# Sorting stage of a graph-attention kernel: transfers spread over two issuing queues, and two instead of four values carried per edge

## The reference, cut to what matters

```
q = (x[src] @ qW); k = (x[dst] @ kW); v = (x[dst] @ vW)      # per edge, 4 heads of 24
e = exp(clip(sum_f q*k, -10, 10))                            # per edge and head
res[n] = sum over edges with src = n of  e / sum(e) * v
out = layernorm(x + (x + res))
```

## Time and profile before

| | us |
|---|---|
| median of 3 runs | 1697.75 (1695.93 to 1699.25) |
| profiled execution, its own time | 1694.7 |
| its span in the profile | 1692.6 |
| PE busy | 1471.8 (87%) |
| DVE busy | 1468.6 (87%) |
| ACT busy | 1013.3 (60%) |
| POOL busy | 1016.2 (60%) |

### The profile page before, as it was taken

One profiled execution on the slowest core, in us unless ns is written; L12 is line 12 of the kernel. 1 busy time (PEld: TensorE's weight loads), 2 busy tenths in 40 slices (PEclk: granted clock), 3 DMA queues, 4 the chain that ended last, 5 costly groups with the idle time before them and its releaser, 6 DMA issues.

```text
span 1692.6 us, 56067 instructions
## 1 busy us (share of the span) xinstructions
PE 1471.8 (87%) x19964; PEld 1414.8 (84%) x19965; DVE 1468.6 (87%) x2980; ACT 1013.3 (60%) x1844; POOL 1016.2 (60%) x764
## 2 busy tenths in 40 slices
PE   4873988899888888898759999999999999999990
PEld 3652888888888888788759999999999999999990
DVE  6988999898898989989148999999999999999987
ACT  3341666566665666666536666666666666666654
POOL 6230777777777777767625555555555555555551
PEclk7565999999999999999979999999999999999995
DMA  5673899999999999999887777777777777777732
GB/s 166 225 273 132 310 373 357 351 334 360 345 364 344 352 351 350 367 318 371 328 297 258 243 242 241 244 246 246 241 244 241 243 245 246 244 241 241 244 113 57
DMA packets 159451, 465.03 MB, mean 275 GB/s; under 512 B 36994, under 2 KB 59266, under 8 KB 152244
## 3 DMA queue, kind: packets, MB, share of 16 engines
q1 hardware_dynamic: 123572, 301.16, 54.5%
q0 software_dynamic: 35840, 163.36, 24.1%
HBM read 271.21 MB, written 209.73 MB: 284 GB/s over the span
## 4 chain that ended last, share of the span: by engine, by line
PE 79%; DVE 9%; issue 7%; SPq 2%; DMA 2%; ACT 1%; POOL 0%; DVEq 0%; POOLq 0%; ACTq 0%
PE two_a L1133 14%; PE meta L1195 13%; PE sum_bank L1195 12%; PE two_b L1133 12%; PE two_a L1216 7%; PE two_b L1216 7%; PE one_c L1206 3%; PE one_d L1206 3%; PE meta L1151 2%; PE one_d L1162 2%; PE sum_bank L1115 1%; SPq L826 1%; DMA work<-kv_table 1%; DVE work L1472 1%; DVE acc L1618 1%
## 5 line engine op out<-in xcount | busy, mean ns | idle before, releaser
L699 POOL TENSOR_TENSOR work<-work 128x768 f32<-128x768 f32 x236 | 452.3, 1917 | 346.4 <-ACT work L941 346.4
L636 POOL DMA_INDIRECT sorted_rows<-work x448 | 501.1, 1118 | 209.6 <-issue 209.0
L1133 PE MATMUL two_a<-work 128*128 128x192 bf16 x2688 | 269.8, 252 | 80.1 <-issue 78.7
L1133 PEld LDWEIGHTS two_a<-work 128*128 128x128 f16 x2688 | 221.1, 100 | 100.8 <-issue 82.4
L904 ACT ACTIVATE work<-two_a 128x768 f32<-128x768 f32 x224 | 181.8, 811 | 179.8 <-PE two_a L1133 179.5
L1133 PE MATMUL two_b<-work 128*128 128x192 bf16 x2688 | 267.1, 251 | 0.0
L950 ACT ACTIVATE work<-work 128x1024 f32<-128x1024 bf16 x236 | 247.5, 1049 | 0.0
L1195 PE MATMUL meta<-work 128*128 128x100 f32 x1888 | 236.9, 279 | 0.9 <-DVE acc L1550 0.9
L1195 PE MATMUL sum_bank<-work 128*128 128x100 f32 x1888 | 235.2, 278 | 0.0
L1583 DVE TENSOR_REDUCE work<-work 128x32 f32<-128x768 f32 x236 | 224.9, 953 | 8.2
L1133 PEld LDWEIGHTS two_b<-work 128*128 128x128 f16 x2688 | 225.5, 100 | 6.7
(11 more groups left out here) (229 smaller groups left out, 2205.8 us busy)
## 6 DMA issues: line engine op xcount, KB each, us to landing
work<-sorted_rows SPq DMA_DIRECT2D x472, 392.0 KB, 3.5
work<-sorted_local SPq DMA_DIRECT2D x56, 1024.0 KB
sorted_rows<-pad_rows SPq DMA_DIRECT2D x49, 392.0 KB, 4.5
work<-kv_table SPq DMA_DIRECT2D x112, 144.0 KB
sorted_rows<-work POOLq DMA_INDIRECT x448
kv_table<-work SPq DMA_DIRECT2D x12, 576.0 KB, 3.4
work<-in_x SPq DMA_DIRECT2D x12, 192.0 KB, 3.8
sorted_local<-work SPq DMA_DIRECT2D x56, 8.0 KB
```

Source lines behind the costliest of these rows:

```text
L636: pool.indirect_dma_start(out=rows_dram, out_offset=bass.IndirectOffsetOnAxis(ap=place_now[:, p, u, b:b + 1], axis=0), in_=payload[:, p, u ...
L699: pool.tensor_tensor(now[:, :, 0:D].rearrange("p c (h f) -> p c h f", h=HEADS), blk[:, k, :, :, D:2 * D].rearrange("p m c (h f) -> p (m c) ...
L1133: mm = pe.matmul(to, picked[:, u % 2, k * P:(k + 1) * P], window[:, u, :, n, :], start=(n == 0), stop=(n == 2))
```

## The change: fewer values, another queue

An edge now carries two values. The tag holds the source's 7 bits plus one and, above them, the target's bits from 10 up; the second value is the low 10 bits of the target's distance from the column's first one. The path on POOL for wide columns puts the target together again from both; it takes more steps than before.

ACT instead of SP now loads the first targets into registers, issues the windows (window `u` right after the evictions of column `u`) and stores the turned rows (right after it has made them). SP issues the broadcast alone.

```diff
-    NV = 4
-    TW = (NV - 1) * NCH
+    NV = 2
+    TW = NV * NCH
...
+            base_regs = [act.alloc_register(f"base{u}") for u in range(QUAD)]
+            act.wait_ge(tables_made, 1)
+            for n in range(2):
+                act.wait_ge(table_out[n], 16 * (TI // 2))
+            act.wait_ge(rest_out, 32)
+
+            def window_of(u, lo):
+
+                act.dma_start(window[:, u].rearrange("p x a b -> p (x a b)"), kv3[bass.ds(lo, P), :]
+                              ).then_inc(window_in[u], 16)
+
             def emit(a, b, c, p=None):
+                following = c is not None and not (isinstance(c, int) and c + 1 >= NQ)
+                if c is None and b == 1:
+                    los = words(act, base_regs, base_i, 0, N - 1)
+                    for u in range(QUAD):
+                        window_of(u, los[u])
+                if following:
+                    los = words(act, base_regs, base_i, times(act, plus(act, c, 1), QUAD), N - 1)
...
-                    act.activation(local_v[:, 0:QUAD * NCH].rearrange("p (u j) -> p u j", u=QUAD), sort_ps[:, :, TW:TW + NCH], ACT.Copy)
+                    act.activation(local_v[:, 0:QUAD * NCH].rearrange("p (u j) -> p u j", u=QUAD), sort_ps[:, :, NCH:TW], ACT.Copy)
...
+                    if not (isinstance(b, int) and b < 2):
+                        act.wait_ge(brow_in, times(act, b, 16, -16))
+                    act.wait_ge(local_rows_made, b1)
+                    act.dma_start(local_dram[bass.ds(low_bits(act, b, 1), 1)].rearrange("o r p -> (o r) p"),
+                                  local_rows[0:QUAD * NCH, :]).then_inc(local_out, 16)
                 if c is not None:
-                    rows(0)
-                    rows(1)
+                    for u in range(QUAD):
+                        rows(u)
+                        if following:
+                            window_of(u, los[u])
...
-            link(dve.tensor_tensor(dst_local, dcol_i, base_ps.unsqueeze(2).to_broadcast([P, NG, COLS]),
+            link(dve.tensor_tensor(dcol_i, dcol_i, base_ps.unsqueeze(2).to_broadcast([P, NG, COLS]),
                                    ALU.subtract))
             link(dve.tensor_copy(base_i[:], base_ps[0:1, :]))
+            link(dve.tensor_copy(base_f[:], base_ps))
...
             def target_parts():
-                link(dve.tensor_single_scalar(bits, dcol_i, (1 << 20) - P, ALU.bitwise_and))
-                link(dve.tensor_copy(dst_hi, bits))
-                link(dve.tensor_single_scalar(bits, dcol_i, P - 1, ALU.bitwise_and))
-                link(dve.tensor_copy(dst_lo, bits))
+                link(dve.tensor_single_scalar(bits, dcol_i, (1 << SPREAD_BITS) - 1, ALU.bitwise_and))
+                link(dve.tensor_copy(dst_near, bits))
+                link(dve.tensor_scalar(dcol_i, dcol_i, SPREAD_BITS, TAG_BITS, ALU.logical_shift_right,
+                                       ALU.logical_shift_left))
...
-                link(dve.tensor_scalar(src_tag, bits, 1.0, None, ALU.add))
+                link(dve.scalar_tensor_tensor(src_tag, bits, 1.0, dcol_i, ALU.add, ALU.add))
...
-                    for v, held in enumerate((src_tag, dst_hi, dst_lo, dst_local)):
+                    for v, held in enumerate((src_tag, dst_near)):
```

More of the change, by code:

```diff
@@ L96, in gnn_program @@
     AW = D + HEADS
-    NV = 4
-    TW = (NV - 1) * NCH
+    NV = 2
+    TW = NV * NCH
+    SPREAD_BITS, TAG_BITS = 10, 8
+    ROUND = 1.5 * 2.0 ** 23
     TI = FULL_NT // TSLOT
@@ L157, in columns @@
             return cols_work[:, n, :].bitcast(F16).rearrange("p (g c) -> p g c", c=COLS)
-        src_tile, src_tag, dst_hi, dst_lo, dst_local, inner = (columns(n) for n in range(6))
+        src_tile, src_tag, dst_near, inner = (columns(n) for n in (0, 1, 2, 5))
         x_all = cols_work[:].rearrange("p a b -> p (a b)")[:, 0:NT * D].rearrange("p (t d) -> p t d", t=NT)
@@ L164, in gnn_program @@
         base_i = sb("base_i", [1, NG], I32)
+        base_f = sb("base_f", [P, NG], F32)
         tile_i = sb("tile_i", [1, FRONT + (JS + 1) * PER_J + 2], I32)
@@ L216, in gnn_program @@
         vals, at = share(at, [GH, NV, NCH, HC], F16)
+        at = max(at, found_end)
         ONEHOTS_END = at
@@ L229, in gnn_program @@
         dst_part, at = share(at, [NCH], F32)
+        far_part, at = share(at, [NCH], F32)
+        tag_part, at = share(at, [NCH], F32)
+        base_part, at = share(at, [NCH], F32)
         place_now, dst_now = place_now.bitcast(U32), dst_now.bitcast(U32)
@@ L645, in fast @@
                     scatter(u, at_c, p)
-            SLOW = 6
+            SLOW = 15
             FAR_COLS = NCH // 2
@@ L658, in slow @@
                     pool.sem_inc(pool_turn, 1)
-                    pool.tensor_tensor(dst_part, here[:, NCH:2 * NCH], here[:, 2 * NCH:3 * NCH], ALU.add
-                                       ).then_inc(slow_step, 1)
+                    pool.tensor_tensor(tag_part, here[:, 0:NCH], one_row[:, 0:NCH], ALU.mult).then_inc(slow_step, 1)
+                    pool.tensor_tensor(dst_part, here[:, NCH:TW], one_row[:, 0:NCH], ALU.mult).then_inc(slow_step, 1)
+                    pool.tensor_tensor(base_part, base_f[:, bass.ds(pool.snap(c * QUAD + u), 1)].to_broadcast([P, NCH]),
+                                       one_row[:, 0:NCH], ALU.mult).then_inc(slow_step, 1)
@@ L661, in slow @@
                     pool.wait_ge(slow_step, made[0])
                     pool.sem_inc(pool_turn, 1)
-                    pool.tensor_copy(dst_now, dst_part).then_inc(slow_step, 1)
-                    pool.wait_ge(slow_step, made[1])
+                    pool.tensor_scalar(far_part, tag_part, 1.0 - P, 2.0 ** -TAG_BITS, ALU.add, ALU.mult
+                                       ).then_inc(slow_step, 1)
+                    pool.wait_ge(slow_step, made[3])
+                    pool.sem_inc(pool_turn, 1)
@@ new lines, in slow @@
+                    pool.tensor_scalar(far_part, far_part, ROUND, None, ALU.add).then_inc(slow_step, 1)
+                    pool.wait_ge(slow_step, made[4])
+                    pool.sem_inc(pool_turn, 1)
+                    pool.tensor_scalar(far_part, far_part, -ROUND, float(1 << SPREAD_BITS), ALU.add, ALU.mult
+                                       ).then_inc(slow_step, 1)
+                    pool.wait_ge(slow_step, made[5])
+                    pool.tensor_tensor(dst_part, dst_part, far_part, ALU.add).then_inc(slow_step, 1)
@@ new lines, in slow @@
+                    pool.wait_ge(slow_step, made[6])
+                    pool.tensor_tensor(dst_part, dst_part, base_part, ALU.add).then_inc(slow_step, 1)
+                    pool.wait_ge(slow_step, made[7])
+                    pool.sem_inc(pool_turn, 1)
+                    pool.tensor_copy(dst_now, dst_part).then_inc(slow_step, 1)
+                    pool.tensor_scalar(far_part, far_part, -(2.0 ** (TAG_BITS - SPREAD_BITS)), None, ALU.mult
+                                       ).then_inc(slow_step, 1)
@@ L665, in slow @@
+                    pool.wait_ge(slow_step, made[9])
+                    pool.tensor_tensor(payload[:, p, u, :, TAG], far_part, tag_part, ALU.add).then_inc(slow_step, 1)
+                    pool.wait_ge(slow_step, made[10])
                     pool.sem_inc(pool_turn, 1)
@@ L676, in slow @@
                                            ).then_inc(slow_step, 1)
-                        pool.wait_ge(slow_step, made[2 * part + 2])
+                        pool.wait_ge(slow_step, made[2 * part + 11])
                         pool.tensor_tensor(to, to, far_rows[:, :, :, 2], ALU.add).then_inc(slow_step, 1)
-                        pool.wait_ge(slow_step, made[2 * part + 3])
+                        pool.wait_ge(slow_step, made[2 * part + 12])
                         pool.sem_inc(pool_turn, 1)
@@ L759, in _ @@
             regs = [sp.alloc_register(f"word{k}") for k in range(PER_J)]
[L760 to L772, removed]
-            def emit(a, b, c, p=None):
[L775 to L782, removed]
+            def emit(a, b, c, p=None):
                 if b is not None:
                     half = bass.ds(low_bits(sp, b, 1), 1)
[L785 to L791, removed]
                     sp.wait_ge(local_out, times(sp, b, 16, 16))
@@ L803, in emit @@
                                  ).then_inc(brow_in, 16)
-                if c is not None and following:
-                    for u in range(1, QUAD):
-                        window_of(u, los[u], at_c)
             first_phase(sp, emit)
```

## The result

The changed kernel takes 1725.05 us (1722.62 to 1730.11, 4 runs) against 1696.84 (1695.56 to 1699.25, 4 runs): ratio 1.0174, 95% interval 1.015 to 1.0198. It is slower by about 28 us, where 1678 us, faster, was forecast.

A forecast was written before the change was run, and what follows sets the result against it. Window 1's wait behind the broadcast was taken to set 12.13 us per group; DMA at 11.8 would follow. Savings of 17.5 + 2.6 + 0 = 20.1 us gave 1678 us, range 1658 to 1712 (8 in 10).

The forecast's parts named there:

- The loop of window 1: Middle stage: window 1's 7.85 us behind the broadcast, column 1's 4.04 and the next issue make 12.1 us per group.
- Two values fewer: DVE saves 0.65 us per group, hidden in the steady stage; 2.6 us gained in the first four groups.
- ACT's turn: Turn of the group: ACT's window issue and register load delay its copies 0.8 us; PE's cycle becomes 11.1 us.
- rival B: ACT's turn becomes the limit, deciding from 1.8 us delay; PE's cycle 12.3, with jitter 12.45; +14 us, 1712; chance 0.22.
- The windows' latency: Windows on ACT's queue take 6 to 7 us; window 1's loop falls to 10.7, window 0 fits up to 7.8.
- C: Window 0, now beside the broadcast, becomes late: 8.2 us latency, loop 12.45 us, +14 us; chance 0.05.
- The clock: Middle stage: PE's longest pauses, with granted clock 0.68 after one, go too; counted inside the 11.8 us period.
- DMA as the next bound at 11.7 to 11.8: Middle stage: 4.24 MB per group at 360 to 363 GB/s takes over; period taken as 11.8 us, saving 17.5 us.
- The rule on the queues: SP and ACT own separate ring rows, DMA engines alternate between rows, so windows on ACT stop standing behind the broadcast.

The follow-up runs named there:

- e9: The kernel before with 16 extra unused matmuls on PE ahead of column 1's window wait: 1701.05 us, 1.0016 of the kernel before.
- e2: The changed kernel with SP's and ACT's old issuing, so only the two values fewer remain: 1693.36 us, 0.9975 of the kernel before.
- f1: The changed kernel without register load on ACT, every window being the table's first 128 rows: 1713.72 us, 1.0113 of the kernel before.
- f2: The changed kernel with registers loaded a group ahead, behind window 0's issue: 1722.6 us, 1.0115 of the kernel before.
- e3: The changed kernel with ACT's register load moved between column 0's evictions and window 0's issue: 1734.44 us, 1.0203 of the kernel before.
- e7: The changed kernel with the 8 KB store given back to SP: 1727.8 us, 1.018 of the kernel before.
- e4: The changed kernel with 12 extra unused matmuls on PE ahead of its turning: 1711.08 us, 1.0079 of the kernel before.
- f3: The changed kernel with two window buffers per column, ACT asking for each window a group earlier: 1689.0 us, 0.9943 of the kernel before.
- f4: Two values; SP loads registers and issues windows a group ahead, ACT issues store and broadcast: 1685.71 us, 0.9925 of the kernel before.
- e1: The kernel before with the queue change alone, four values still carried: 1726.64 us, 1.0158 of the kernel before.
- g1: The changed kernel with SP holding each broadcast until window 0 has landed, on a slower chip: 2059.42 us, 1.0257 of the kernel before.
- g2: Register load behind window 0's issue, plus 14 idle matmuls ahead of column 0's window wait, slower chip: 2065.43 us, 1.0307 of the kernel before.
- e5: Two values, SP issuing as before except the broadcast, which ACT issues between evictions of columns 0 and 1: 1694.51 us, 0.9974 of the kernel before.
- e6: Two values, all issues on SP, two window buffers per column, windows asked a group earlier: 1696.45 us, 0.9991 of the kernel before.
- section 3: Experiments asking for windows a group ahead with two buffers per column: issued by ACT 1689.0 us, all issues on SP 1696.45 us.

## Why the prediction was wrong, by its own steps

- **What bounds the kernel before: right.** The loop of window 1 behind the broadcast was there; with the windows on another queue its wait is gone (25.2 us to none for column 1), and with the pause filled (e9) the period does not fall (12.26 us).
- **Two values fewer: right.** L1466's 1.30 us became L1488's 0.69; e2 measured -4.2 us (-2.5 to -6.1), where 2.6 were put. Nothing came of it in the steady stage.
- **ACT's turn: right in kind, a little under.** Sequencer work does go on beside a running eviction (L896 at 503.07 inside the eviction from 502.94). The load took 1.30 us in that group. L926 came 2.42 us after the last eviction's start instead of 0.82; PE's wait is 1.0 us per group on average, where 0.8 was put. It stayed under the 1.8 us from which rival B was to decide. Taking it away brings little or nothing: f1 has 1.0113 and f2 1.0115 (to 1.0187) for 1.0174, e3 1.0203.
- **The windows' latency: this step failed.** I took 6 to 7 us and let window 0 fit up to 7.8. The middle was right, 7.0 us, but I worked with one value where there is a spread: window 0 needs over 7.8 us in 17 of 47 groups, 8.10 and 9.26 in the chain above, and in none of 49 before. What I did not carry through is the order of issue. SP's own sequence had put window 0 ahead of the broadcast; with the window on ACT nothing does, and it goes out 1.6 us behind one (median). That the store left SP is not the reason, for e7 has the same. I gave C 0.05, with +14 us.
- **The clock: this step failed too.** I wrote "PE's longest pauses go too" and priced it inside the 11.8. They moved to the turn of the group, where the wait at the turning and window 0's wait stand a few small matmuls apart. The stage's clock fell from 0.96 to 0.91. In the sum of PE's time this is the whole 0.66 us a group; what a test gives back is half, 14 of 28 us (e4), and e3 loses as much at 0.94. Both B and C had their own length as price and no clock: C's loop was to be 12.45 us with 4.04 for the column, and one is 14.2 with 5.9. B's wait and C's also came in one kernel, B's in every group and C's in 21 of 46 (over 0.3 us), and I had priced each alone. So the 28 us lie beyond both.
- **DMA as the next bound at 11.7 to 11.8: not reached here.** Where the windows are no longer late, the wait goes to the scatter at 348 to 350 GB/s and a period of about 12.05 (f3, f4). The 362 GB/s of f1's first third, at 11.8 us a group, were not held to the end by any kernel.
- **The rule on the queues.** The Trainium skill, page "DMA: Bandwidth & Descriptors", section "Queues, rings and completion order", let me expect that a window on ACT's row does not stand behind a broadcast. The traces agree for window 1 (7.4 us became 5.1). For window 0, which now shares the DMA engines with a broadcast from its start, the median rose from 6.3 to 7.0 and the longest from 7.0 to 10.4. I had read the rule for the one transfer that gains.

Shown: the loss is in the queue change (e1, e2), it goes when the windows are asked for a group earlier (f3), the store has no part in it (e7), and filling the pause at the turn gives back 14 us while the clock rises to 0.98 (e4). Argued from the traces and not tested: that window 0 is late because it is issued just behind a broadcast. The distances above and g1's two windows speak for it; g2's speak less so, and e5, with nearly as many slow windows and no loss, suggests that a slow window 0 does harm only together with something else at the turn. How much is the register load's stays open, since e3, f2 and f1 differ. Nor is it settled which pauses lower the clock; that the two waits in a row do it is read from single groups.

## What to carry to other kernels

Moving transfers to another queue changes the order in which all of them start. Follow each one to its consumer, the ones that were early too: what was ahead of a large transfer may now be behind it. When a wait moves, look at what PE does around its new place. Here PE's total wait stayed about the same, and the matmuls behind its new place ran at the lower clock in 23 of 46 groups, where it had been 9 of 49. The old place was not free of it either, as the row of 0.68 behind a pause of 2.6 us shows. Where the latency of a small load sets the period, a second buffer can be worth more than another queue: it brought 0.9943 for 1.0174 here with the windows on ACT (f3). With everything on SP it brought nothing (e6, 0.9991 for e2's 0.9975), where the store then became the late one.

## What the runs showed of the hardware that was not expected

- The granted clock was 0.50 in the 6.4 us with and behind the second of two waits, 0.80 and 2.65 us long and 0.5 us apart. It stayed at 1.00 behind one of 2.0 us, and was 0.68 behind one of 2.6 us.
- Giving PE 12 useless matmuls per group made the kernel 14 us faster (1711 for 1725). In the kernel before, 16 raised the clock too (0.96 to 0.99) and the time stayed (1.0016).
- A 144 KB window issued less than 2 us behind a 1024 KB broadcast on the other queue needed 7.7 us (median of 28), one 2 to 5 us behind it 5.3 us (of 15).
- A load of two registers on ACT took 0.56 us in one group and 1.30 us in the group before it, from the same table (0.49 to 2.04 us over 56 loads).
- On two chips the kernel before took 1956 and 2018 us instead of 1697, and the differences between kernels there are not those of the others: f3's kernel was 2.3% slower than the kernel before on the first of them (1.4 to 3.2%) and 0.6% faster on the chip of section 3.
